# A Mamba-plus-FFN layer on one Trainium2 core: early scaling in two passes, decode turns in the FFN's banks, codes cast by GpSimd's transfers

## What is computed

```python
def mamba(u):                        # W_in 1160x512, conv_w 640x1x4, W_out 512x512, 8 heads, state 64
    z, x, B, C, dt = split(u @ W_in.T, [512, 1024, 1088, 1152])
    x, B, C = split(silu(causal_conv4(concat(x, B, C)) + conv_b), [512, 576])
    dt = softplus(dt + dt_bias); dA = exp(-exp(A_log) * dt)
    S[t] = S[t-1] * dA[t] + dt[t] * outer(x[t], B[t]); y[t] = S[t] @ C[t]
    return ((y + D_param * x) * silu(z)) @ W_out.T

def ffn(x):                          # gate_idx, up_idx 1376x512, down_idx 512x1376, values 0..15
    return (silu(x @ lut[gate_idx].T) * (x @ lut[up_idx].T)) @ lut[down_idx].T

x = x + layernorm(mamba(layernorm(x)))
x = x + layernorm(ffn(layernorm(x)))
```

## Time and profile before

| | |
|---|---|
| median of 3 executions | 1568.88 us |
| the profiled execution | 1568.46 us, its span 1566.7 us |
| PE busy | 1421.7 us (91%) |
| DVE, ACT, POOL busy | 931.1 (59%), 636.4 (41%), 453.5 us (29%) |
| PE busy in 40 slices, tenths | 2668888788799999999999999998999899999999998 |
| masks L1441 | 320, 111.3 us, mean 407 ns |
| decode matmuls L1154 | 640, 130.5 us |
| codes, SP's queue | 80 transfers of 208 KB, median 3.4 us to landing |
| code casts of ACT | 40 |

### The profile page before, as it was taken

One profiled execution on the slowest core, in us unless ns is written; L12 is line 12 of the kernel. 1 busy time (PEld: TensorE's weight loads), 2 busy tenths in 40 slices (PEclk: granted clock), 3 DMA queues, 4 the chain that ended last, 5 costly groups with the idle time before them and its releaser, 6 DMA issues.

```text
span 1566.7 us, 20158 instructions
## 1 busy us (share of the span) xinstructions
PE 1421.7 (91%) x7392; PEld 710.4 (45%) x7392; DVE 931.1 (59%) x1877; ACT 636.4 (41%) x1078; POOL 453.5 (29%) x689
## 2 busy tenths in 40 slices
PE   2668888788799999999999998999899999999998
PEld 1234444344445544455444544455455454444443
DVE  6666865587547654675557644775476546534333
ACT  4356555566544433343433433343434322232220
POOL 1032221332223243334233332334133424310201
PEclk9879998899999999999999999999999999999999
DMA  5022211321000021001110111012101110110101
GB/s 151 22 75 69 69 58 58 96 68 60 27 28 28 21 68 48 28 21 54 35 54 21 41 48 41 14 34 74 41 14 35 54 35 14 61 61 14 54 1 47
DMA packets 36626, 72.13 MB, mean 46 GB/s; under 512 B 5808, under 2 KB 5808, under 8 KB 36528
## 3 DMA queue, kind: packets, MB, share of 16 engines
q1 hardware_dynamic: 34640, 70.81, 14.3%
q10 hardware_dynamic: 1888, 0.03, 0.1%
HBM read 54.05 MB, written 16.78 MB: 45 GB/s over the span
## 4 chain that ended last, share of the span: by engine, by line
PE 67%; issue 13%; DVE 11%; ACT 4%; DMA 3%; POOL 2%; SPq 0%; ACTq 0%; POOLq 0%; DVEq 0%
PE bank L1244 22%; PE bank L1100 15%; PE bank L1258 11%; PE bank L1154 4%; PE bank L1204 4%; DVE mask L1441 3%; DVE xs L1470 2%; PE bank L1187 2%; PE bank L1200 2%; PE bank L1210 2%; DMA ut<-u 2%; DMA conv_b_sb<-conv_b 1%; PE bank L1111 1%; PE bank L1178 1%; DVE decay L1528 1%
## 5 line engine op out<-in xcount | busy, mean ns | idle before, releaser
L1244 PE MATMUL bank<-fxt,ffn_hi 128*128 128x512 f16 (+1 forms) x1408 | 428.0, 386 | 21.6 <-DVE gact L1589 19.2
L1244 PE MATMUL bank<-fxt,ffn_lo 128*128 128x512 f16 (+1 forms) x704 | 271.9, 386 | 0.0
L1244 PEld LDWEIGHTS bank<-fxt,ffn_hi 128*128 128x128 f16 (+1 forms) x1408 | 141.0, 101 | 196.9 <-DVE gact L1589 21.6
L1154 PE MATMUL bank<-mask,diag 128*128 128x416 f16 x640 | 130.5, 360 | 30.9 <-ACT yt L797 13.6
L562 POOL TENSOR_TENSOR state<-state,ex 64x512 f32<-64x512 f32 x32 | 36.0, 1126 | 408.4 <-PE bank L1200 408.4
L1441 DVE TENSOR_SCALAR mask<-codes_h 128x832 f16<-128x832 f16 x320 | 111.3, 407 | 52.5 <-PE bank L1154 51.0
L1589 DVE SCALAR_TENSOR_TENSOR gact<-gact,bank 128x512 f32<-128x512 f32 (+1 forms) x88 | 60.2, 684 | 127.9 <-ACT gact L814 127.0
L1258 PE MATMUL bank<-ffn_hi,h_hi 128*128 128x512 f16 (+1 forms) x352 | 133.5, 379 | 0.0
L1258 PE MATMUL bank<-ffn_hi,h_lo 128*128 128x512 f16 (+1 forms) x352 | 133.4, 379 | 0.0
L1258 PE MATMUL bank<-ffn_lo,h_hi 128*128 128x512 f16 (+1 forms) x352 | 133.3, 379 | 0.0
L814 ACT ACTIVATE gact<-bank,c_gate_half 128x512 f32<-128x512 f32 (+1 forms) x88 | 60.0, 682 | 158.6 <-PE bank L1244 158.6
(11 more groups left out here) (172 smaller groups left out, 2480.7 us busy)
## 6 DMA issues: line engine op xcount, KB each, us to landing
codes_sb<-codes SPq DMA_DIRECT2D x80, 208.0 KB, 3.4
ures<-u SPq DMA_DIRECT2D x32, 256.0 KB, 2.8
x_scratch<-x SPq DMA_DIRECT2D x32, 256.0 KB, 2.0
ut<-x_scratch SPq DMA_DIRECT2D x16, 512.0 KB, 3.5
xres<-x_scratch SPq DMA_DIRECT2D x32, 256.0 KB, 2.8
out<-dn SPq DMA_DIRECT2D x32, 256.0 KB, 2.1
ut<-u SPq DMA_DIRECT2D x15, 512.0 KB, 3.9
ffn_hi<-w_in_t SPq DMA_DIRECT2D x4, 580.0 KB, 9.7
```

The costliest lines, as they stand in the source:

```text
L1154: last = nc.tensor.matmul(p.bank[:, 0:COLS], diag[:, q].rearrange("p n m -> p (n m)"), mask[:, n, q, j * COLS:(j + 1) * COLS], start=(q == ...
L1244: last = nc.tensor.matmul(bank, wt[:, c0:c0 + w], fxt[:, half, k, :], start=(k == 0 and n == 0), stop=(k == KC - 1 and n == 2))
```

## The change

It has five parts.

- **Two passes for the maxima.** DVE reduces the table first (its scale is made on each partition alone, without the all-reduce), then `w_in`; POOL's all-reduce now covers `w_in` only and the scale is made at once. The maximum of `w_out`, a second all-reduce and its scale follow after the third low half and after the first gate. `conv_b` is loaded second on ACT's queue with a semaphore of its own.
- **Order of the prologue.** PE projects X4 ahead of dt and the z blocks of tile 0 between the X blocks. The first convolution keeps its sums in `x1`, and the last convolution's input lies in `xsplit`. The high and low half of `w_out` come late. The 16 diagonals become one POOL operation of 128x1024 elements.
- **Banks.** z0 to z3 of tile 0 and all decode turns leave the ring of two and form a ring of their own over the banks 3, 6 and 7.
- **Codes.** POOL issues the 80 transfers, which cast int32 to float16 and write `codes_h` directly; SP's transfers, `codes_sb` and ACT's casts are gone. A unit from the fourth on waits until the masks have read its slot.
- **Masks.** They compare with `pair_code[:, q]`, 2q on the lower partitions and 2q+1 on the upper.

```diff
-        return ["T0", "T1", "T2", "T3", "dt", "X4", "X0", "X1", "X2", "X3", "z0", "z1", "z2", "z3", "sN"]
+        return ["T0", "T1", "T2", "T3", "X4", "dt", "X0", "X1", "X2", "X3", "sN"]
...
-    return (d(0) + n("T0", "T1") + ["s1"] + d(1) + ["y0"] + d(2) + ["o0"] + n("T2", "T3") + d(3, 4)
-            + d(5) + n("dt", "X4") + ["s2"] + d(6) + ["y1"] + n("X0") + d(7) + ["o1"] + d(8, 9)
-            + d(10) + n("X1") + ["s3"] + d(11) + n("X2") + ["y2"] + n("X3") + d(12) + ["o2"] + d(13, 14)
-            + d(15) + n("z0") + n("sN") + d(16) + f("F0", "F1") + ["y3"] + d(17) + n("z1") + ["o3"]
-            + d(18) + f("F2") + n("z2", "z3") + d(19) + f("F3"))
+    return (n("T0", "T1") + ["s1", "y0", "o0"] + n("T2", "T3") + n("dt", "X4") + ["s2", "y1"] + n("X0")
+            + ["o1"] + n("X1") + ["s3"] + n("X2") + ["y2"] + n("X3") + ["o2"] + n("z0", "sN")
+            + f("F0", "F1") + ["y3"] + n("z1") + ["o3"] + f("F2") + n("z2", "z3") + f("F3"))
+def early_turns():
+    return [(-1, f"z{c}") for c in range(SUB)] + [(t, f"D{k}{j}") for t in range(LAG) for k in range(SUB * STEP) for j in "ab"]
...
+    first_turns = early_turns()
+    for i, turn in enumerate(first_turns):
+        place_of[turn] = (2 + i % len(FFN_BANKS), i // len(FFN_BANKS))
+    TURN_BANKS = (0, 1) + FFN_BANKS
...
+                def load_codes(k):
+                    if k >= HALF_UNITS:
+                        return
+                    if k >= CODE_SLOTS:
+                        pool.wait_ge(s_masks, 2 * (k - CODE_SLOTS + 1))
+                    cols = slice(k // 2 * UNIT, (k // 2 + 1) * UNIT)
+                    for copy in range(2):
+                        pool.dma_start(codes_h[copy * NST:(copy + 1) * NST, k % CODE_SLOTS, :],
+                                       codes_blocks[:, k % 2, cols]).then_inc(s_codes[k % CODE_SLOTS], 16)
...
                     decay_state(t, 0)
                     segments(t, 1)
+                    load_ahead(3, 4)
                     if t >= 1:
                         out_rstd(t - 1, 3)
                         add_residual(t - 1, 3)
                     weights(t, 1)
+                    load_ahead(5)
                     if nxt:
                         pair_rstd("u", t + 1, 1)
+                    load_ahead(6, 7)
                     decay_state(t, 1)
                     segments(t, 2)
+                    load_ahead(8, 9)
                     out_rstd(t, 0)
                     add_residual(t, 0)
                     weights(t, 2)
+                    load_ahead(10, 11)
                     if t >= 1:
                         pair_rstd("x", t - 1, 0)
+                    load_ahead(12)
                     decay_state(t, 2)
                     segments(t, 3)
+                    load_ahead(13, 14)
                     out_rstd(t, 1)
                     add_residual(t, 1)
                     weights(t, 3)
+                    load_ahead(15, 16, 17)
                     decay_state(t, 3)
                     if nxt:
                         segments(t + 1, 0)
+                    load_ahead(18, 19)
                     if g >= 0:
                         down_rstd(g, 0)
                     out_rstd(t, 2)
...
-                pool.wait_ge(s_big, KC + 3)
-                nc.gpsimd.partition_all_reduce(big[:], lowest[:], P, RMAX).then_inc(s_all, 1)
+                for k in range(CODE_SLOTS):
+                    load_codes(k)
+                pool.wait_ge(s_lowest, 1)
+                nc.gpsimd.partition_all_reduce(big[:, 0:1], lowest[:, 0:1], P, RMAX).then_inc(s_all, 1)
+                pool.wait_ge(s_sel, 2 * 2 + 1)
+                nc.gpsimd.tensor_tensor(
+                    diag[:], fold[:].unsqueeze(1).unsqueeze(1).broadcast_to((P, PAIRS, 2, NST)),
+                    lut_sel[:].rearrange("p n q -> p q n").unsqueeze(3).broadcast_to((P, PAIRS, 2, NST)),
+                    ALU.mult).then_inc(s_diag, 1)
+                pool.wait_ge(s_wbig, 1)
+                nc.gpsimd.partition_all_reduce(big[:, 1:2], lowest[:, 1:2], P, RMAX).then_inc(s_wall, 1)
...
-                        dve.wait_ge(s_half, count + 1)
+                        dve.wait_ge(s_codes[count % CODE_SLOTS], 32 * (count // CODE_SLOTS + 1))
                     if q == 0 and count >= 2:
                         dve.wait_ge(s_masks_used, count - 1)
                     if q == GROUP and count >= 2:
                         t, k = divmod(count - 2, SUB * STEP)
                         p = place(t, f"D{k}b")
                         dve.wait_ge(p.filled, p.n + 1)
-                    ins = nc.vector.tensor_scalar(mask[:, n, q, :], codes_h[:, count % CODE_SLOTS, :], float(2 * q), None,
+                    ins = nc.vector.tensor_scalar(mask[:, n, q, :], codes_h[:, count % CODE_SLOTS, :], pair_code[:, q:q + 1], None,
...
+                dve.wait_ge(s_lut, 16)
+                step(nc.vector.tensor_reduce(big[:, 2:3], lut_sb[:], AX_X, ALU.max, apply_absolute_value=True))
+                scales(2)
...
+                nc.vector.tensor_reduce(lowest[:, 0:1], win_max[:], AX_X, ALU.max).then_inc(s_lowest, 1)
+                dve.wait_ge(s_all, 1)
+                scales(0)
+                step(nc.vector.tensor_scalar(c_in[:], expo[:, 0:1], 1.0 / (XS * WS), None, ALU.mult))
+                nc.vector.tensor_scalar(c_in_half[:], c_in[:], 0.5, None, ALU.mult).then_inc(s_scale, 1)
...
+                for n in range(3):
+                    low_half(n)
+                dve.wait_ge(s_wout, 16)
+                nc.vector.tensor_reduce(lowest[:, 1:2], w_out_f, AX_XY, ALU.max,
+                                        apply_absolute_value=True).then_inc(s_wbig, 1)
                 clear_state(0)
+                dve.wait_ge(s_alog, 1)
+                step(nc.vector.tensor_scalar(a_sb[:], a_sb[:], -1.0, None, ALU.mult))
                 conv(0, 4)
+                dt_input(0)
+                conv(0, 0)
+                conv_silu(0, 4)
+                conv_silu(0, 0)
                 time_steps(0)
-                conv_silu(0, 4)
-                conv(0, 0)
                 conv(0, 1)
-                conv_silu(0, 0)
                 conv(0, 2)
                 conv_silu(0, 1)
                 conv(0, 3)
                 conv_silu(0, 2)
                 conv_silu(0, 3)
-                for c in range(SUB):
-                    z_gate(0, c)
+                z_gate(0, 0)
+                dve.wait_ge(s_wall, 1)
+                scales(1)
+                nc.vector.tensor_scalar(c_out[:], c_in[:], expo[:, 1:2], 0.25 / (WS * WS), ALU.mult,
+                                        ALU.mult).then_inc(s_wscale, 1)
+                weigh(0, 0)
+                z_gate(0, 1)
+                decayed(0, 0)
+                low_half(3)
+                step(nc.vector.tensor_scalar(c_gate_half[:], expo[:, 2:3], 0.5 / (XS * WS), None, ALU.mult))
+                step(nc.vector.tensor_scalar(c_down[:], expo[:, 2:3], expo[:, 2:3], 32.0 / WS, ALU.mult, ALU.mult))
+                step(nc.vector.tensor_scalar(c_down[:], c_down[:], expo[:, 2:3], None, ALU.mult))
+                z_gate(0, 2)
                 masks(0)
-                weigh(0, 0)
-                decayed(0, 0)
+                z_gate(0, 3)
                 masks(1)
...
                 pe.wait_ge(s_lo, 2)
+                all_transposed(-1, "T2")
+                all_transposed(-1, "T3")
+                project_conv(0, 4)
                 project_dt(0)
-                for f in CONV_ORDER:
-                    project_conv(0, f)
+                project_conv(0, 0)
+                project_conv(0, 1)
                 pe.wait_ge(s_lo, 3)
-                for c in range(SUB):
-                    project_z(0, c)
+                project_z(0, 0)
+                project_conv(0, 2)
+                project_z(0, 1)
+                project_conv(0, 3)
+                project_z(0, 2)
                 prepare(0, 0)
                 segment_sums(0, 0)
+                project_z(0, 3)
```

225 lines of the change are left out of this document (73 added, 152 removed).

## The result

The changed kernel took 1556.96 us (median of 4, 1556.23 to 1559.38) against 1568.76 before: a ratio of 0.9929, 95% interval 0.9912 to 0.9947, 11.8 us faster. The forecast was 25.4 faster, to 1544; 1557 still lies in its range of 1522 to 1578. The direction was right, and the second ring is what made the kernel faster, but the size was not: under half of what was forecast arrived.

What follows compares the result with a forecast made beforehand. The prediction saw PE as busy for 91%, with time to win in the prologue and stages 0 and 1, DVE bounding chunks 1 and 2. Terms -6 - 3.2 - 17.2 + 1 = -25.4 gave 1544 us, range 1522 to 1578.

Steps and rivals of the forecast that it cites:

- Prologue, -6: Start to first scan result: an earlier first scale and shorter waits bring that result from 87.03 to about 81 us.
- I take 0: Prologue, POOL: going from the six transfer issues to the first all-reduce costs nothing; upper bound 3.8 us for both all-reduces.
- I take 3.6 us: Prologue, behind the first convolution's start: own sum and input buffers and two dropped ACT casts shorten waits by 3.6 us.
- from there to the first scan result I count nothing: Prologue's end, after the x half: earlier z blocks set against second scale, weighing and late low half, net 0.
- The ring, 31.2 before the pointer: Stages 0 and 1: decode turns in own banks give back 12.0 us in chunks 1 and 2, 19.2 in first and last.
- the first chunks' 10.1: First chunks of stages 0 and 1: PE's out-projection no longer waits for `ffn_lo`, saving 4.8 and 5.3 us.
- their split is ready at 118.47 + 0.69 = 119.16, just in time: 4.8 go: Stage 0's first chunk: transposes behind the earlier out-projection could come at 119.2 with their split ready, saving 4.8 us.
- DVE as the bound in chunks 1 and 2: Stages 0 and 1: the ring returns DVE's 12.0 us of waits, the pointer takes 8.8, net -3.2 us.
- The pointer, 8.8 + 2.0 = 10.8: Masks' pointer operand: 0.055 us each on DVE, costing 8.8 us in chunks 1 and 2, 2.0 in first and last chunks.
- The issues, +1: POOL's code transfers: 1.0 us per issue, four just hidden by a 4.2 us cover; +1 us for chunks with less cover.
- The rival in which POOL becomes the bound: Chunks: issues beside masks cost much more than SP's, from 1.84 us each erasing the gain; 1580 to 1618; chance 0.15.
- The rival with all ring waits gone and a better clock: Stages 0 and 1: all 49 us of ring waits go and PE is granted more than 0.90 clock; 1522; chance 0.10.

Runs made afterwards that it cites:

- run 4: Changed kernel with POOL's first six code-transfer issues behind the first all-reduce instead of in front of it: 1556.30 us, ratio 0.9921.
- run 5: Changed kernel with the first two units of masks moved into DVE's waits at the prologue's end, ahead of the first scan result: 1551.96 us.
- run 6: Changed kernel with both edits of run 4 and run 5 together: 1551.12 us, ratio 0.9889.
- run 3: Changed kernel with the codes' old path (SP's transfers, ACT's casts, masks comparing with immediates), banks and prologue new: 1550.58 us, ratio 0.9881.
- run 2: Kernel before with only the second ring (banks 3, 6, 7 for tile 0's z blocks and the decode turns): 1551.99 us, ratio 0.9888.
- run 8: Kernel of run 2 with first-chunk DVE statistics ahead of unit 3's masks and ACT's out-projection copy ahead of the second pair's normalisation: 1552.50 us.
- run 12: Kernel of run 2 with 16 extra matmuls in PE's wait for the first split, in each of stages 0 and 1: 1543.17 us.
- run 7: Changed kernel with only the decode turns put back into the shared ring of two banks: 1579.40 us, ratio 1.0072.
- run 15: Kernel of run 14 with ACT's copy of the first chunk's out-projection ahead of unit 2's weights: 1532.06 us, ratio 0.9770.
- run 10: Kernel of run 3 with run 5's mask order and run 8's earlier statistics, without run 8's moved copy: 1539.00 us, ratio 0.9814.
- run 1: Changed kernel with masks comparing with an immediate instead of the pointer operand (odd codes' masks left out): 1548.49 us, ratio 0.9866.
- run 11: Changed kernel with 56 and 20 extra matmuls in PE's wait for the first split of stages 0 and 1: 1548.29 us, ratio 0.9868.
- run 14: Kernel of run 10 with 40 and 20 extra matmuls in PE's wait for the first split of stages 0 and 1: 1531.12 us, ratio 0.9763.

## Why the prediction was wrong

- **What bounds the kernel** was read rightly: nothing moved in the rest (1130.8 and 1131.9), and the time came from stages 0 and 1. Of the 13.6 us that are missing, 4.9 are the prologue's and 6.8 the first chunks', which gain as little in runs 4 to 6 (0.8 to 3.9 of 10.1).
- **Prologue, -6: failed, it gave 1.1.** Three steps of it. "I take 0" for what POOL needs from an issue to the all-reduce: 2.95 us passed between input and run, 2.0 more of DVE's wait than before. The upper bound that was written down, 3.8, held it; runs 4 and 3 show that it is the issues in front. Then "I take 3.6 us" for the shorter waits between the first convolution and the end of the x half: that stretch gained 1.9, of 1.5 ahead at its start and 3.4 at its end. No run here takes it apart. And "from there to the first scan result I count nothing": 64.6 to 85.9 takes 21.3 us, where 68.0 to 87.0 took 19.0, because gates of z, which had been the wait before, were replaced by waits for `gram`, `decay` and the last high half, with the masks queued behind them. Run 5 moves the masks into those waits (3.7), run 6 both (6.0, first result at 79.93). What z in banks of its own brings, 2 to 4 in the old order (runs 2, 8 and 12), was set against the late low half as equal; the new order's waits were the larger.
- **The ring, 31.2 before the pointer: mis-sized.** The direct test, run 2, is 16.8 faster in all, 2 to 4 of it in the prologue. Taken back alone from the change the decode turns are worth 22.4 (run 7). The term that is too large in both is the first chunks' 10.1: 4.0 in run 2, 4.8 in run 7, 3.3 in the change. The step that failed is "their split is ready at 118.47 + 0.69 = 119.16, just in time: 4.8 go". The split was near (119.8), but the second transposes need the bank of the out-projection, and ACT copies that only after it has waited for POOL's statistics, normalised twice and copied unit 2: they start at 121.77 and not at 119.2 or a little later. Behind them the decoding ran 2.0 us slower at a lower clock, and 16 slower masks stand in front of the scan result. That the copy alone sets the chunk is not shown: runs 8 and 15 take its wait away and are no faster. That the chain in front of it counts (statistics behind masks on DVE, POOL's roots, ACT, DVE's split) is what run 10 supports, by the 6 to 7 us that it leaves for the statistics.
- **DVE as the bound in chunks 1 and 2: not borne out.** The change gained 2.2 there for a forecast of 3.2 (7.5 with the chunks of runs 4 to 6). But of the 12.0 for DVE's waits run 2 shows 5.4 and runs 8 and 12 some 3.3, while run 7, among the slower masks, shows 10.1; and the 8.8 for the pointer don't show there in run 1. So the sum was near, its two terms were not, and what bounds these chunks no run takes apart.
- **The pointer, 8.8 + 2.0 = 10.8: the size was near**, 8.5 (run 1), at 0.067 a mask for 0.055, **the place was luck**. It was to cost 8.8 in chunks 1 and 2 and 2.0 elsewhere; run 1 shows 2.9 at most there, and 3.1 in the first chunk of stage 0 alone, where masks stand in front of the statistics and in front of the scan result.
- **The issues, +1: the price was too high**, 0.56 for 1.0, and the path is worth 2 us rather than costing 1 (run 3 against run 1). Its lower bound of 0.745 was SP's first four transfers; SP's 80 have a median of 0.596. The rival in which POOL becomes the bound is refuted. (That rival's "masks (0.3 each, 312) fill 106" should read 94; nothing hangs on it.) By the sentence of the Trainium skill ("SBUF — State Buffer", section "A bandwidth-pool intuition that's wrong (but worth ruling out)") a GpSimd transfer that takes about 620 ns alone takes about 3100 ns beside a DVE `tensor_copy`, which the prediction took for the price of an issue. No row here shows that stall beside masks. Twelve of the 80 issues lie wholly beside masks and took 0.6 to 0.7 us each; the longest of all took 0.757, and the 74 in the chunks landed 2.6 to 3.9 us after their issue. The masks were slowed as well. By the timelines of POOL and DVE, in chunk 1 of stage 0, with a POOL multiplication beside the same masks, eight took 3.68 for 2.85:

```profile
148.95 1.44 POOL L493 DMA_DIRECT2D codes_h<-codes  x2
...
147.98 3.68 DVE L1431 TENSOR_SCALAR mask<-codes_h,pair_code 128x832 f16<-128x832 f16 x8
```

- **The rival with all ring waits gone and a better clock** had the clock's sign wrong: fewer waits, but one of 14.5 us among them, and 0.87 over 80 to 424 us where it was 0.90.
- **The sum.** From before, by medians: the second ring -16.8 (run 2), the new prologue -1.4 (run 3 against 2), POOL's path -2.1 (run 1 against 3), the pointer +8.5 (the change against run 1), -11.8 together. The steps of 1.4 and 2.1 are within the spread of runs; that the pointer takes back half of the ring is not.

## What to carry to other kernels

A wait that a resource causes is worth what is left after the next thing in line, and the next thing may be an in-order engine that is far from busy: follow the buffer's whole way back, to the instruction that frees it and what is queued in front of it there. A cast that a transfer can do is free only if nothing else pays: here the comparison took 0.067 us a time, eight times a unit, to save a 0.97 us operation on an engine (ACT) that is busy for 41% of the time in the kernel before. And put filler work (masks of the next unit) where the engine waits, not in front of the result that others wait for.

## What the runs showed of the hardware that was not expected

- A matmul whose result is thrown away can make a kernel faster: 76 of them in two waits brought 8.7 us in the changed kernel, 32 brought 6.9 in the kernel before. After PE had stood for 14.47 us, its work of the next 8.3 us ran at a granted 0.50; with the wait filled the same work ran at 1.00 in 4.7 (run 11). The 32 decode matmuls later in the chunk, behind waits of 3.58 and 2.55, took 7.8 us, and 8.1 with the first wait filled; where the clock was granted in full throughout the chunk (1.00, run 14), behind one wait of 2.93, they took 5.79.
- The times of one kernel go with that clock: in run 14 the mean granted clock of five executions is 0.975, 0.972, 0.971, 0.966, 0.971 for 1525.5, 1530.3, 1532.0, 1539.6 and 1531.1 us.
- Between GpSimd's last transfer issue and its all-reduce lie 5.89 us without a row, and 7.51 between the all-reduce and the `tensor_tensor` behind it, the last 5.9 of them with all inputs written. The second pause doesn't come from the issues: in run 3, where POOL issues none, it is 7.75. A pause of this kind hides only where POOL has nothing to do: the second all-reduce, behind 9.14 us of waiting, ran 0.14 us after its input.
- Transfers that cast int32 to float16, issued by GpSimd, cost it 0.54 us each in the median and landed in 2.8 us, against 0.60 of SP's queue and 3.4 for the int32 ones.
